# Row maxima as pairs of narrow matmuls, with scores and pairs in three PSUM slots in turn

## What is computed

```python
# layer 0, per image: standard heads, and two wide ones
scores = jnp.einsum('bhqd,bhkd->bhqk', qh, kh) / math.sqrt(hd)          # hd = 16, 8 heads
standard_out = jnp.einsum('bhqk,bhkd->bhqd', softmax(scores), vh)
sc = jnp.einsum('bqd,bkd->bqk', qm, km) / math.sqrt(64)                 # twice
parts.append(jnp.einsum('bqk,bkd->bqd', softmax(sc), vm))
# layer 1: attention over the tokens, 8 heads of 16; then top-2 of 8 experts
dots = jnp.einsum('bhqd,bhkd->bhqk', q, k) * 16 ** -0.5
out = jnp.einsum('bhqk,bhkd->bhqd', softmax(dots), v)
```

## Time and profile before

| | |
|---|---|
| median of 3 runs | 3155.28 us (3152.79 to 3157.88) |
| the profiled execution | 3174.35 us, its span 3172.6 us |
| TensorE matmul | busy 2801.3 us, 88% of the span |
| VectorE | 2156.5 us, 68% |
| ScalarE | 1680.1 us, 53% |
| POOL | 564.5 us, 18% |
| mean granted TensorE clock | 0.943 of 2.4 GHz |

### The profile page before, as it was taken

The page is one execution under the profiler, slowest core; times in us unless marked ns, Lnnn a source line. Parts: engine busy times, 40 slices in busy tenths (PEclk is TensorE's granted clock), DMA queues, the critical chain, the costliest instruction groups (busy, mean ns, idle before and its releaser), DMA issues. The chain is left out here.

```text
span 3172.6 us, 41798 instructions
## 1 busy us (share of the span) xinstructions
PE 2801.3 (88%) x14912; PEld 1136.2 (36%) x14912; DVE 2156.5 (68%) x4191; ACT 1680.1 (53%) x2470; POOL 564.5 (18%) x499
## 2 busy tenths in 40 slices
PE   3897799989999899998999898998999989998945
PEld 1122223363234433263233632344332632336234
DVE  4665878568774887668785687747876687856620
ACT  1363356556565466555565565654655555655623
POOL 4000021014010230103210140102301023101222
PEclk9698799999999999998999999998999999999957
DMA  4001220172104530163202721045301542017024
GB/s 110 1 2 33 46 50 8 57 208 55 28 15 137 135 67 2 54 184 78 38 11 67 201 49 28 18 136 133 67 2 54 173 79 48 10 62 195 22 80 144
DMA packets 155230, 229.16 MB, mean 72 GB/s; under 512 B 24368, under 2 KB 72432, under 8 KB 154912
## 3 DMA queue, kind: packets, MB, share of 16 engines
q1 hardware_dynamic: 146848, 209.78, 26.0%
q0 software_dynamic: 8192, 16.79, 2.0%
HBM read 174.29 MB, written 52.20 MB: 71 GB/s over the span
## 5 line engine op out<-in xcount | busy, mean ns | idle before, releaser
L1359 DVE TENSOR_REDUCE blockmax<-ps 128x1 f32<-128x512 f32 x1952 | 1282.2, 684 | 399.4 <-PE ps L723 347.8
L1170 ACT ACTIVATE prob<-ps 128x1024 f32<-128x1024 f32 x1024 | 998.1, 1022 | 617.6 <-PE ps L896 599.3
L723 PE MATMUL ps<-ks,qs 96*128 96x512 bf16 x1696 | 659.6, 407 | 156.3 <-DVE blockmax L1359 108.7
L896 PE MATMUL ps<-qs,ks 99*128 99x512 bf16 x2048 | 628.2, 392 | 1.8 <-ACT prob L1170 0.7
L723 PEld LDWEIGHTS ps<-ks,qs 96*128 96x128 bf16 x1696 | 156.8, 99 | 780.5 <-DVE blockmax L1359 633.9
L1217 ACT ACTIVATE prob<-ps,b1t 128x128 f32<-128x128 f32 x736 | 209.7, 368 | 168.3 <-PE ps L1006 168.2
L913 PE MATMUL ps<-prob,va_b 128*32 128x512 f32 x2048 | 283.7, 627 | 5.3 <-ACT prob L1170 5.3
L913 PE MATMUL ps<-prob,va_a 128*32 128x512 f32 x2048 | 277.2, 613 | 0.0
L896 PEld LDWEIGHTS ps<-qs,ks 99*128 99x128 bf16 x2048 | 189.6, 100 | 234.1 <-issue 70.8
L605 POOL TENSOR_TENSOR rs<-vn,vec 128x1 f32<-128x1 f32 (+1 forms) x40 | 40.2, 1006 | 1290.8 <-DVE vn L1308 885.1
L1370 DVE TENSOR_REDUCE blockmax<-ps 128x2 f32<-128x1024 f32 x176 | 207.1, 1221 | 50.7 <-PE ps L753 49.9
(11 more groups left out here) (229 smaller groups left out, 3055.7 us busy)
## 6 DMA issues: line engine op xcount, KB each, us to landing
parts_dram<-parts SPq DMA_DIRECT2D x32, 768.0 KB, 4.8
ks<-parts_dram SPq DMA_DIRECT2D x192, 128.0 KB, 4.3
qs<-parts_dram SPq DMA_DIRECT2D x192, 128.0 KB, 6.2
shared<-in_w SPq DMA_DIRECT2D x96, 256.0 KB, 3.2
prob<-in_w SPq DMA_DIRECT2D x96, 256.0 KB, 3.2
routed<-in_w SPq DMA_DIRECT2D x80, 256.0 KB, 3.4
xe<-in_w SPq DMA_DIRECT2D x48, 256.0 KB, 3.2
oatt<-in_w SPq DMA_DIRECT2D x48, 256.0 KB, 3.0
```

The lines of the kernel that those rows point to most:

```text
L723: pe.matmul(ps[:, MX + n % 2, :], qs[0:ROWS, slot, h, tile * P:(tile + 1) * P], ks[0:ROWS, slot, h, cols(k)], start=True, stop=True).then_ ...
L896: mm = pe.matmul(ps[:, SC + h, :], ks[:, slot_of(a, g), h, t * P:(t + 1) * P], qs[:, slot_of(a, g), h, cols(q)], start=True, stop=True)
L1170: act.activation(prob[:, n % 3, 2 * pr:2 * pr + 2, :], ps[:, SC + 2 * pr:SC + 2 * pr + 2, :], ACT.Exp, scale=HD ** -0.5).then_inc(exp_done ...
L1359: dve.tensor_reduce(blockmax[:, unit_of(j), cell_of(j), k:k + 1], ps[:, MX + n % 2, :], AX.X, ALU.max).then_inc(blocks_used[f], 1)
```

## The change

Every block maximum becomes one of a pair of matmuls on the high bf16 parts alone, 32 rows each for two heads that lie side by side (64 rows each for the two wide heads). One reduce of 1024 columns serves a pair. `HEAD_BLOCKS`, `UNIT` and the families count pairs. 22 pairs of `a0` are made a stage ahead (64 blocks before), so 58 pairs of `a1` stand in the conv stage (96 blocks before), 42 of `b` and 22 of `a0` in the token stage: two per step, in steps 0 to 28 and 0 to 31. In a step TensorE issues both calls of scores, the weighing of the step before, then both pairs, then the small products. Scores and pairs share three slots of two banks: call 0 of step n takes slot n, call 1 slot n + 1, the pairs slots n + 2 and n + 3, all modulo three. So call 0 waits for both exponentials of the step before, call 1 for the first pair of the step before to be reduced, pair 0 for its second, pair 1 for the first exponential of its own step. VectorE reduces both pairs at the start of a step and then does the step's small work.

For the keys of odd heads and for the queries that are overwritten too soon, POOL makes copies (`keep_parts_b`, `k_even_a`, `k_odd_a`) in buffers that are free then, and ScalarE waits for them before it writes the next parts. The windows shift by a step or so, and on SP unit 2 of `b` goes ahead of the query parts, unit 3 behind the copies of the second group.

```diff
+        def slot_banks(i):
+            first = (SC, SC + 2, MX)[i % 3]
+            return ps[:, first:first + 2, :]
...
+            def max_pair(a, n, i, f, d, run):
+                if i == 0 and n:
+                    pairs_used(a, n - 1)
+                elif i == 0 and a == 1 and run:
+                    pe.wait_ge(blocks_used["b"], EARLY)
+                elif i == 1 and run:
+                    pe.wait_ge(exp_done[a], 2 * n + 1)
+                banks = slot_banks(n + 2 + i)
...
+                h, t, k = pair_of(d)
+                tile = unit_of(d) % 2 * NT // 2 + t
+                q_high = (q_high_a, q_kept_b)[f == "b"]
+                k_high = ((k_even_a, k_odd_a), (k_even, k_odd_b))[f == "b"][unit_of(d) // 2]
+                for j in range(2):
+                    rows = slice(32 * (h + j), 32 * (h + j + 1))
+                    mm = pe.matmul(banks[:, j, :], q_high[rows, tile * P:(tile + 1) * P], k_high[rows, cols(k)],
+                                   start=True, stop=True)
+                mm.then_inc(blocks_ready[f], 1)
...
             def scores(a, n, pr):
-                if n >= 1:
-                    pe.wait_ge(exp_done[a], 2 * (n - 1) + pr + 1)
+                if n >= 1 and pr == 0:
+                    pe.wait_ge(exp_done[a], 2 * n)
+                elif n >= 1:
+                    first_pair_used(a, n - 1)
...
-            def attention_step(a, n, blocks, run):
+            def attention_step(a, n, pairs, run):
+                if run:
                     scores(a, n, 0)
                     scores(a, n, 1)
                 if run and n:
                     weigh_values(a, n - 1)
+                for i, (f, d) in enumerate(pairs):
+                    max_pair(a, n, i, f, d, run)
...
+            def reduce_pair(f, d, banks):
...
                 dve.wait_ge(blocks_ready[f], n + 1)
+                dve.tensor_reduce(cells, banks, AX.X, ALU.max).then_inc(blocks_used[f], 1)
+                if d % UNIT == UNIT - 1:
+                    close_unit(f, d)
...
+            def keep_parts_b():
+                pool.wait_ge(done["k_even"], 1)
+                pool.tensor_tensor(k_odd_b, parts[:, 0, 0, :], k_even[:, :], ALU.subtract).then_inc(done["k_odd_b"], 1)
+                pool.wait_ge(done["q1_b"], 2)
+                pool.tensor_copy(q_kept_b, parts[:, 1, 0, :]).then_inc(done["q_kept_b"], 1)
...
-TOKEN_WINDOW = {1: ["pre"], 4: ["turn_b_1"], 5: ["norm"], 8: ["kA0"], 9: ["kA1"], 10: ["qA0"], 11: ["qA1"],
+TOKEN_WINDOW = {3: ["pre"], 5: ["turn_b_1"], 7: ["norm"], 9: ["kA0"], 10: ["kA1"], 11: ["qA0"], 12: ["qA1"],
```

More of the change, by code:

```diff
@@ L108 @@
 SLOT_PAIRS = 2
[L109 removed]
+TURN_PAIR = UNIT
 BETWEEN_PAIRS = {0: "tg4", 7: "tg5", TURN_PAIR: "turn_b_0"}
@@ L114, with conv_pairs, token_pairs, unit_of @@
 SLOTS = TILES + 2
[L115 to L155, removed]
+assert SLOT_PAIRS * (SLOTS - PAIR_SLOT) == EARLY
+def conv_pairs(n):
+    first = EARLY + STEP_PAIRS * n
+    return [("a1", d) for d in range(first, first + STEP_PAIRS)] if n < CONV_PAIR_STEPS else []
+def token_pairs(n, token, front):
+    first = EARLY + STEP_PAIRS * n
+    if n < TOKEN_PAIR_STEPS:
+        return [("b", d) for d in range(first, first + STEP_PAIRS)] if token else []
+    return [("a0", d - HEAD_PAIRS) for d in range(first, first + STEP_PAIRS)] if front else []
+def unit_of(d):
+    return d // UNIT
+def pair_of(d):
+    r = d % UNIT
+    if d < HEAD_PAIRS:
+        return r % 2 * 2, r // 4, r // 2 % 2
+    return 0, r // 2, r % 2
 def slot_of(a, g):
@@ L268, in build @@
         k_even = sb("k_even", [P, S], BF16)
+        k_odd_b, q_kept_b = (keysum[:, m, :].bitcast(BF16) for m in range(MULTI))
+        k_even_a, k_odd_a = mrow, parts[:, 0, 0, :]
+        q_high_a = parts[:, 1, 0, :]
         rows_x = [prob[:, 0, 2 + k, :] for k in range(2)]
@@ L729, in multi_block, with multi_pair @@
+            def multi_pair(d, banks):
+                _, t, k = pair_of(d)
+                if d == HEAD_PAIRS:
                     pe.wait_ge(small_free, small["km1"])
                     pe.wait_ge(small_free, small["qm1"])
-                rows = slice(MD * m, MD * (m + 1))
-                pe.matmul(ps[:, MX + n % 2, :], qmh[rows, t * P:(t + 1) * P], kmh[rows, cols(k)],
-                          start=True, stop=True).then_inc(blocks_ready["a1"], 1)
+                for m in range(MULTI):
+                    rows = slice(MD * m, MD * (m + 1))
+                    mm = pe.matmul(banks[:, m, :], qmh[rows, t * P:(t + 1) * P], kmh[rows, cols(k)],
+                                   start=True, stop=True)
+                mm.then_inc(blocks_ready["a1"], 1)
@@ L1070, in small_product @@
                     i, h = "kq".index(name[0]), int(name[2])
+                    if token:
+                        act.wait_ge(done[("k_odd_b", "q_kept_b")[i]], 1)
                     read_small(parts[:, i, 0, cols(h)], ps[:, SM, :], name, f"{name[0]}1_a")
@@ L1653, in attention_step @@
                     last[0] = n
-                while stream and stream[0][0] <= n:
-                    reduce_next()
-                for name in now:
+                for name in extra:
                     small_product(name)
+                    last[0] = n
             if experts or conv:
-                late = []
                 if conv:
-                    stream.extend((n, b) for n in range(2 * STEPS) for b in conv_blocks(n))
+                    stream.extend((n, (f, d, slot_banks(n + 2 + i))) for n in range(2 * STEPS)
+                                  for i, (f, d) in enumerate(conv_pairs(n)))
                 for n in range(2 * STEPS):
-                    names = small.conv.get(n, ())
-                    attention_step(n, late + (CONV_EXTRA.get(n, []) if experts else []), names[:-1])
-                    late = list(names[-1:])
+                    attention_step(n, small.conv.get(n, ()), CONV_EXTRA.get(n, []) if experts else [])
             if conv:
```

201 lines of the change are left out of this document (94 added, 107 removed).

## The result

The changed kernel takes **3233.61 us** (median of 4 runs, 3230.13 to 3235.18) against 3154.03 in the same session: 1.024 times as long, 95% interval 1.021 to 1.027. The forecast was 3175, or +0.6%: right in sign and inside the whole range (3075 to 3270), but outside its own range (3130 to 3220), and the loss is four times as large as forecast. Execution against execution, the profiled one after took 3235.03 us (span 3233.2), the one before 3174.35: +60.7.

A forecast was written before the change was run, and what follows sets the result against it. TensorE was taken as the bound before, a TensorE-VectorE loop of 3.32 us a step after. Conv +62 and +3, token -100 and -1, first block -16 make -52; clock +72 gives +20: 3175 us, own range 3130 to 3220, whole 3075 to 3270.

The forecast's parts named there:

- The loop: Each attention step with pairs: pair 0, its reduce, scores 1, weighing, next pair 0 close a cycle of 3.32 us.
- scores of step 16 wait: 4.9: Conv steps 12 to 16: logits, split and routes make the row maxima late, so scores of step 16 wait; 4.9 us.
- The 2.69 of scores 0: Steps without pairs: scores 0 waits for the second exponential instead of the first, 2.69 us a step.
- rival (d): The pairs don't run together in their new place: 0.21 us more a step, 3272 us; chance 0.03.
- Rival (b): TensorE's saving of 33 us an iteration and 16 comes out in full: 2908 us; chance 0.06.
- Conv, +8.8 a stage at full clock: Conv stage: loop steps plus VectorE's excess work give 117 us against 108.1; seven times, +62.
- Token, -14.3 a stage at full clock: Token stage: loop steps plus waits and other extras give 122.5 us against 136.8; seven times, -100.
- First block: First block: 22 pairs where 64 blocks were made, no wait for spread keys; -12 to -20 us, taken -16.
- Rival (a): The clock stays up, so the sum holds without the clock terms: 3103 us; chance 0.27.
- the clock term: Slower steps at 1.2 GHz: 41 us at stage starts, 31 behind the token wait, together +72.
- Rival (c): The clock falls for good in many steps; with a third of 461 pair steps at 1.2 GHz, 3334 us; chance 0.14.
- The step to the median: Whole kernel: the +20 found from the profiled execution of 3174.35 us was put on the median 3155.28, giving 3175.

## Why the prediction was off, and what in it was right

The loop, the pairs and the places of most waits were right; the forecast was 59 us short because the waits for late results were mis-sized, because one of them stands on another path than predicted, and because of the base that the sum was put on. The step that failed is, above all, the conv term "scores of step 16 wait: 4.9".

**What bounds the kernel, and the loop: right.** VectorE's reduce and TensorE's order close the loop; 3.25 us measured for 3.32, each part within 0.08. The half reduce (2.71) and the pair ahead of the weighing (3.03) changed it as a loop through the reduce must. The 2.69 of scores 0 came out as 2.70 in the last steps of the last token stage, which have no pairs. That TensorE ran almost without a gap before is true of the conv stage (106 of 109.5 us) and less of the token stage (123 of 137.5).

**The pairs run together: right.** Four matmuls end 0.40 us after the first begins, as in the earlier trace rows; rival (d) is out. Rival (b) is out by the loop: TensorE works 196 us less and none of it shows.

**Conv, +8.8 a stage at full clock: the step that failed.** With the start's clock the sum was 119.6, measured 123.1. The scores of step 16 do not wait for rows (0.4 us in one stage of eight). TensorE stood before that, 4.1 us at `km1` in step 14: the turn's result lies in the bank of the small products, so a late split holds up the next product, and with it all that TensorE has to do behind it. For the earlier trace rows I had summed how long VectorE's work is, not where TensorE stands while it goes on. From step 10 to step 16 (by first exponentials) the seven stages take 7.5 to 9.2 us more than six plain steps, mean 8.5, for 4.9: 3.6 a stage, or 25 us in seven, about what the conv stages missed in all (26). Part of it goes with the clock, which the sum put at nothing there: from step 12 to 16 it is 7.9 to 8.2 over plain in the four stages where the granted clock was 0.84, and 6.9 to 7.0 in the three where it was 0.91. From step 22 to 25 the mean was 6.2 for 5.0, from step 6 to 10 5.8 for 4.9; that the loop was 0.07 shorter than predicted took 2 back.

**Token, -14.3 a stage at full clock: near by luck.** The stall before step 8 was named with its cause; 8.1 us over a plain step for 7.2, the first key product 5.9 for 4.3, the 3x3 products 5.1 for 3.1. Step 16 failed: 1.8 (0 to 4) predicted, 4.6 measured, and 2.4 more in the step behind it (granted 0.68), for nothing. I counted SP as busy with six copies, not that the row's first transfer then takes its way behind them: 4.55 us from the first issue to the second, where unit 1 took 1.39 and the earlier trace rows 1.43. Against that, the 4.5 for the clock behind the wait of step 8 was too much: the steps 8 and 10 took 0.4 and 0.7 over plain. The 0.2 in the sum has no row behind it. Errors of both signs left 2 us a stage.

**First block: right** in kind, -22 for -16, just outside its bounds (-12 to -20).

**The clock: right in kind, too dear in sum.** Granted 0.91 in both stages; that is 0.18 of their time at 1.2 GHz, behind stage starts and waits as said. Rival (a) is out by that. The price of a step was right: token step 2 took 4.77 us in the five stages where its granted clock was 0.50, and 3.25 in the two where it was 0.81 and 0.87; 4.8 and 3.32 were predicted. By the mean granted clocks TensorE had 1.2 GHz for some 490 us of the span, 360 before; at the price of a step the 130 us between them cost some 40 (an estimate), for +72 in the sum. So the clock term covered a part of what the waits lacked. Rival (c) is out by the plain steps, which keep 2.4 GHz although TensorE stands still in each. Four of them, in the last token stage:

```profile
3018.15:3031.15 13.00, 9.87 (x69) 1.94 (x65) 9.43 (x8) 8.59 (x9) 2.41 (x2) 1.00 0.01 1
```

By the rule that I cited from the Trainium skill, "TensorE: Matmul & The Clock Gate", section "A second HAM failure mode: psum-queue depth-cycling", the clock would have gone up and down in these steps; the trace does not agree.

**The step to the median: failed by itself.** The sum came out of one execution of 3174.35 us, and I put its +20 on the median of 3155.28. Execution against execution it is +20 for +60.7, on the medians +20 for +79.6. The 19 us between them go with the clock: over the other executions of the kernel before, those of 3147 to 3155 us have a mean granted clock of 0.948 to 0.953, those of 3174 to 3189 one of 0.938 to 0.944. A place where it shows in the trace is the start of the conv stages: two of the seven took 105.5, the others up to 109.5, and the difference lies in the first steps. First 10 us of one of each kind, before the change:

```profile
1212.90:1222.90 10.00, 9.71 (x59) 3.48 (x57) 9.08 (x22) 7.05 (x8) 0.00 (x0) 1.00 0.01 2
1581.10:1591.10 10.00, 9.85 (x33) 3.12 (x30) 5.75 (x13) 4.66 (x5) 0.00 (x0) 0.56 0.01 2
```

After the change the profiled execution lies 1.4 us from its median. That an execution of the median has fewer of these starts at the lower clock is argued, not shown. So the miss of 59 us is 26 for the conv stages, 14 for the token stages and 9 between the stages (for which there was no term), less 3 for the first conv and the last token stage and 6 for the first block, together 40; and 19 for the base.

**What would show it** came as listed, steps of 3.25 us, reduces of 1.22, scores 1 released by a reduce, the stall before token step 8, conv stages longer and token stages shorter; but the stage lengths missed by waits that a new order of the small work takes away, not by the loop.

## What to carry to other kernels

An order of small work by hand, here laid out for steps of 3.4 and 4.3 us, has its deadlines in steps: the pairs, the slots and the order in a step that cost 2.4% with the old order took 2.0% off with a new one. Price a late result by everything that stands behind its buffer (here one PSUM bank), not only by its reader. Look at the steps with extra work before a gain in the plain step is multiplied by all steps. And put a sum made from one execution against that execution.

## What had not been expected of the hardware

TensorE's clock fell after a wait of 2.6 us although it worked without a gap from then on: 1.7 us at 2.4 GHz, then a stretch at 0.60 of it (the run with extra products in both waits). Where the extra products took the place of the wait, before conv step 24, the step ran at 1.00 instead of 0.52. Two pair matmuls of 32 rows alone hold TensorE as long as four together, 0.32 us (the run with the first pair ahead). A two-step transfer of one row took 1.39 us from issue to issue alone and 4.55 behind six copies of 128 KB each.
